# Cross-attention loop with queries turned by VectorE and transfers, projected two steps ahead, and probabilities normalised on ScalarE

## The reference, cut to what matters

```python
x = x + _L0_xattn_ref(_layernorm(x), ctx_2048, mask, ...)   # 16 batches, 128 queries, 128 keys, width 512
x = x + _L0_ffn_ref(_layernorm(x), ...)                     # routed block on 16 rows of each batch
...
q = (hidden_states @ Wq + bq)      # 16 heads of 128
k = (encoder_hidden_states @ Wk + bk); v = ... @ Wv + bv    # 4 heads of 128, each used by 4 query heads
q = _rmsnorm(q, qn_w); k = _rmsnorm(k, kn_w)
scores = einsum('bhsd,bhed->bhse', q, k) / sqrt(128) + attention_mask
out = einsum('bhse,bhed->bhsd', softmax(scores), v)
return out @ Wo
```

## Time and profile before

| | before |
|---|---|
| median of 3 timed runs | 835.98 us (832.25 to 836.52) |
| the profiled execution's own time | 833.15 us |
| its span, first to last instruction | 831.4 us |
| granted TensorE clock, mean | 0.983 of 2.4 GHz |
| busy TensorE, VectorE, ScalarE, GpSimd | 787.2, 566.4, 470.7, 548.3 us |

### The profile page before, as it was taken

The page is one execution under the profiler, slowest core; times in us unless marked ns, Lnnn a source line. Parts: engine busy times, 40 slices in busy tenths (PEclk is TensorE's granted clock), DMA queues, the critical chain, the costliest instruction groups (busy, mean ns, idle before and its releaser), DMA issues. The chain is left out here.

```text
span 831.4 us, 14178 instructions
## 1 busy us (share of the span) xinstructions
PE 787.2 (95%) x3968; PEld 654.6 (79%) x3968; DVE 566.4 (68%) x1049; ACT 470.7 (57%) x1618; POOL 548.3 (66%) x611
## 2 busy tenths in 40 slices
PE   6999996999999999999999999999987799989997
PEld 4888874888888888888888888888865577877886
DVE  4545455687787787787787787778777688754122
ACT  4555455575675675675665665665654256554440
POOL 2333355677777777776776876876867297756980
PEclk9999997999999999999999999999999899999999
DMA  7666663222322332332332332332254655213620
GB/s 231 200 212 205 200 218 97 60 82 68 103 83 68 102 90 64 101 91 67 95 95 63 96 94 63 98 91 63 76 158 155 231 186 182 103 54 125 204 99 25
DMA packets 85001, 97.66 MB, mean 117 GB/s; under 512 B 8112, under 2 KB 48176, under 8 KB 84976
## 3 DMA queue, kind: packets, MB, share of 16 engines
q1 hardware_dynamic: 84400, 95.52, 37.6%
q0 software_dynamic: 576, 1.84, 0.6%
HBM read 63.77 MB, written 17.30 MB: 98 GB/s over the span
## 5 line engine op out<-in xcount | busy, mean ns | idle before, releaser
L900 POOL TENSOR_TENSOR wp_lo<-raw,wp_hi 128x512 fp32r<-128x512 f32 x88 | 113.9, 1336 | 34.8 <-ACT wp_hi L970 34.8
L1080 ACT ACTIVATE p_row<-s_row,neg_max 128x128 f32<-128x128 f32 x256 | 100.0, 395 | 63.8 <-DVE neg_max L1374 63.7
L824 POOL TENSOR_TENSOR p_row<-p_row,p_inv 128x512 f32<-128x512 f32 x64 | 66.8, 1044 | 98.1 <-DVE p_inv L1389 98.1
L1794 PE MATMUL b_y<-wo_hi,oT_hi 128*128 128x512 f32 x256 | 107.5, 420 | 3.4 <-DVE oT_lo L1278 3.4
L1796 PE MATMUL b_y<-wo_hi,oT_lo 128*128 128x512 f32 x256 | 101.8, 398 | 0.0
L1795 PE MATMUL b_y<-wo_lo,oT_hi 128*128 128x512 f32 x256 | 101.8, 398 | 0.0
L1794 PE MATMUL b_q<-wq_hi,xT_hi 128*128 128x512 f32 x248 | 97.8, 394 | 0.0
L1796 PE MATMUL b_q<-wq_hi,xT_lo 128*128 128x512 f32 x248 | 97.4, 393 | 0.0
L1795 PE MATMUL b_q<-wq_lo,xT_hi 128*128 128x512 f32 x248 | 97.3, 392 | 0.0
L970 ACT ACTIVATE oT_hi<-b_o 128x512 fp32r<-128x512 f32 x64 | 38.4, 599 | 102.2 <-PE b_o L1796 100.3
L856 POOL TENSOR_TENSOR pT_lo<-raw,pT_hi 128x512 fp32r<-128x512 f32 x62 | 81.0, 1307 | 0.9 <-ACT pT_hi L970 0.9
(11 more groups left out here) (369 smaller groups left out, 2206.3 us busy)
## 6 DMA issues: line engine op xcount, KB each, us to landing
raw<-raw SPq DMA_DIRECT2D x248, 64.0 KB, 2.1
cx<-in_ctx_dram SPq DMA_DIRECT2D x16, 256.0 KB, 2.7
raw<-in_L_xattn_Wq_dram SPq DMA_DIRECT2D x16, 256.0 KB, 2.7
raw<-in_L_xattn_Wo_dram SPq DMA_DIRECT2D x16, 256.0 KB, 3.2
v_store<-v_out SPq DMA_DIRECT2D x16, 256.0 KB, 3.3
k_store<-k_out SPq DMA_DIRECT2D x16, 256.0 KB, 2.0
xr<-in_x_dram SPq DMA_DIRECT2D x16, 256.0 KB, 3.1
v_raw<-v_store SPq DMA_DIRECT2D x16, 256.0 KB, 3.0
```

What stands on the lines that cost most here:

```text
L824: pool.tensor_tensor(p_row[:], p_row[:], per_head(p_inv, S), ALU.mult).then_inc(p_normed, 1)
L900: last = pool.tensor_tensor(wp_lo[n % NSLOT][:, c, :], raw[RAW_OF[n]][:, c, :], wp_hi[n % NSLOT][:, c, :].bitcast(fp32), ALU.subtract)
L1080: e = act.activation(place, row, ACT.Exp, bias=neg_max[:, h:h + 1], accum_out=p_sum[:, h:h + 1])
L1794: pe.matmul(dst, left[0], right[0], start=start, stop=False)
```

## The change

On TensorE `turn_q` stays for batch 0 only. From quad 4 on, GpSimd's `q_norm` multiplies in place in `q_row`; VectorE's new `q_turn` transposes blocks of 32 x 32 from `q_row` to `q_nrm`; four DMAs of SyncE (`load_q`) put the blocks into one of two places; ScalarE's `loaded_q_high` and GpSimd's new `q_low` split from there. The weight qw moves into the keys' weight. `project_q` works on quad t + 2. The multiplication of the probabilities (`p_norm`) goes from GpSimd (one instruction) to ScalarE (four). x is normalised in place, and `turn_x`, `x_high` and `x_low` move from i = 2 to i = 1. Within a step the order of each queue changes.

```diff
@@ keys are loaded in the layout of the values; SyncE
+                sp.dma_start(k_raw[:], k_store[bass.ds(b * P, P), :].rearrange("(j d) n -> d j n", j=4)
...
+            def load_q(t, par):
+                sp.wait_ge(q_turned, t + 1)
+                for i in range(4):
+                    sp.dma_start(qT_in[par][:, i].rearrange("p h s -> p (h s)"),
+                                 q_tr[32 * i:32 * i + 32].rearrange("d j h s -> d j (h s)")
+                                 ).then_inc(qT_loaded, 16)
...
+                    if (i == NQUAD - 1 or not first) and (i < NQUAD - 1 or not last):
+                        load_q(t + 1, (i + 1) % 2)
                     if not (first and i == 0) and not (last and i == NQUAD - 1):
                         load_p(t - 1, (i - 1) % 2)
@@ GpSimd
+                    pool.tensor_tensor(q_row[:], q_row[:], per_head(q_rs, HD), ALU.mult).then_inc(q_normed, 1)
...
+            def q_low(t, par):
+                pool.wait_ge(qT_hi_done, t + 1)
+                pool.tensor_tensor(by_head(qT_lo), qT_in[par].rearrange("p i h s -> p h i s"),
+                                   by_head(qT_hi).bitcast(fp32), ALU.subtract).then_inc(qT_lo_done, 1)
...
-                    if i == 1 and not last:
+                    if i == 1 and first:
                         x_norm_stat(b + 1)
-                    if i == 2:
+                    if i == 2 and first:
                         v_low(b)
+                    if i < NQUAD - 1 or not last:
+                        q_norm(t + 1)
+                    if i == 1 and not first and not last:
+                        x_norm_stat(b + 1)
                     if i == NQUAD - 1 and not first:
                         out_stat(b - 1)
...
-                    if not (first and i == 0):
+                    if not first:
+                        q_low(t, i % 2)
+                    if i == 2 and not first:
+                        v_low(b)
+                    if last and i == NQUAD - 1:
                         p_norm(t - 1)
                     if not (first and i < 2):
                         p_low(t - 2, i % 2)
-                    if not (first and i < NQUAD - 1) and not (last and i == NQUAD - 1):
-                        q_norm(t + 1)
@@ ScalarE
+            def loaded_q_high(t, par):
+                act.wait_ge(qT_loaded, 64 * (t - NQUAD + 1))
+                wait(act, scored, t)
+                copy(by_head(qT_hi), qT_in[par].rearrange("p i h s -> p h i s")).then_inc(qT_hi_done, 1)
...
+            def p_norm(t):
+                act.wait_ge(p_inverted, t + 1)
+                for h in range(QUAD):
+                    last = act.activation(p_row[:, h, :], p_row[:, h, :], ACT.Copy, scale=p_inv[:, h:h + 1])
+                last.then_inc(p_normed, 1)
...
+                    else:
+                        loaded_q_high(t, i % 2)
...
                         exps(t - 1, last and i == NQUAD - 1)
+                    if i == 2:
+                        v_high(b)
                     if not (first and i < 2):
                         p_high(t - 2, i % 2)
-                    if i == 2 and not last:
+                    if i == 1 and not last:
                         x_high(b + 1)
...
+                    if not (first and i == 0) and not (last and i == NQUAD - 1):
+                        p_norm(t - 1)
+                    if not (first and i < 2) and not (last and i >= 2):
+                        squares(t + 2)
                     if i == NQUAD - 1 and not last:
                         k_high(b + 1)
@@ VectorE
+            def q_turn(t):
+                dve.wait_ge(q_normed, t + 1)
...
+                    dve.wait_ge(qT_loaded, 64 * (t - NQUAD))
+                dve.transpose(q_tr, q_row[:].rearrange("p h (j d) -> p j h d", j=4)).then_inc(q_turned, 1)
...
+                    if (i == NQUAD - 1 or not first) and not (last and i == NQUAD - 1):
+                        q_turn(t + 1)
+                    if not (first and i < 2) and not (last and i >= 2):
+                        q_bias(t + 2, (i + 2) % NQUAD, b_y if first and i == 2 else b_q)
                     if not (first and i == 0):
                         p_invert(t - 1)
...
-                        q_bias(t + 1, (i + 1) % NQUAD)
...
-                        q_low(t)
@@ TensorE
-                        project_q(t + 1, b if i < NQUAD - 1 else b + 1, (i + 1) % NQUAD)
-                    turn_q(t)
+                    if first:
+                        turn_q(t)
...
+                    elif not (last and i >= 2):
+                        project_q(t + 2, b if i < 2 else b + 1, (i + 2) % NQUAD, banks=2 if first else 1)
-                    if i == 2 and not last:
+                    if i == 1 and not last:
                         turn_x(b + 1)
```

More of the change, by code:

```diff
@@ L243, in xattn_then_routed_ffn @@
             tied = sb_in(st, "tied", [P, 1])
+        qT_in = [row.rearrange("p (i h s) -> p i h s", i=4, h=QUAD) for row in (raw[1][:, 3, :], q_in1[:])]
         wo_place.close()
@@ L634, in _ @@
             load_v(0)
-            sp.wait_ge(x_normed, 1)
+            sp.wait_ge(x_turned, 1)
             load_x(1)
@@ L1093, in attend @@
                         o_high(t - 3)
-                    if i == 2:
-                        v_high(b)
-                    if (first and i < NQUAD - 1) or (last and i == NQUAD - 1):
+                    if first:
                         q_high(t)
+                    else:
+                        loaded_q_high(t, i % 2)
                     if first and i < NQUAD - 1:
@@ L1350, in q_bias @@
                 dve.wait_ge(q_projected, t + 1)
-                wait(dve, q_normed, t)
+                if isinstance(t, int) and t <= NQUAD:
+                    wait(dve, q_normed, t)
+                else:
+                    dve.wait_ge(q_turned, t)
                 dve.tensor_tensor(q_row[:].rearrange("p h d -> p (h d)"), bank[:],
@@ L1489, in attend @@
                         norm_out(b - 1)
-                    if first and i == 1:
-                        q_bias(3, 3)
-                    if not (first and i < NQUAD - 1) and not (last and i == NQUAD - 1):
-                        q_bias(t + 1, (i + 1) % NQUAD)
-                    if not (first and i < NQUAD - 1) and not (last and i == NQUAD - 1):
-                        q_low(t)
-                    if i == 2 and not last:
+                    if i == 1 and not first and not last:
                         x_low(b + 1)
-                    if first and i == 1:
-                        dve.wait_ge(w_hi, 2 * NB)
-                        dve.wait_ge(w_lo, 2 * NB)
-                    if not (first and i == 0) and not (last and i == NQUAD - 1):
+                    if not (first and i < 2) and not (last and i == NQUAD - 1):
                         p_turn(t - 1)
@@ L1525, in attend @@
                     s_max(t)
-                    if first and i == 0:
-                        q_bias(2, 2, b_y)
+                    if first and i == 1:
+                        x_low(b + 1)
+                        dve.wait_ge(w_hi, 2 * NB)
+                        dve.wait_ge(w_lo, 2 * NB)
+                        p_turn(t - 1)
+                    if first and i < 2:
+                        q_bias(i + 2, i + 2, (b_y, b_q)[i])
             attend(0, True, False)
@@ L1821, in turn_x @@
                 wait(pe, xT_lo_done, b)
-                turn(b_xT, xn).then_inc(x_turned, 1)
+                turn(b_xT, xr).then_inc(x_turned, 1)
             def kv_project(bank, par, w_hi_, w_lo_, split_at=None):
@@ L1947, in attend @@
                         find_places(0)
[L1948 to L1950 removed]
+                    if first:
+                        turn_q(t)
                     if first and i < 2:
                         project_q(i + 2, 0, i + 2, (b_y, b_q)[i], banks=2)
[L1953 removed]
+                    elif first and i == 2:
+                        project_q(t + 2, b + 1, 0, b_y, banks=2)
+                    elif not (last and i >= 2):
+                        project_q(t + 2, b if i < 2 else b + 1, (i + 2) % NQUAD, banks=2 if first else 1)
+                    if i == 1 and not last:
                         turn_x(b + 1)
```

41 lines of the change are left out of this document (19 added, 22 removed).

## The result

| | before | changed |
|---|---|---|
| median of the timed runs | 836.25 us (4 runs, 832.25 to 837.84) | 907.80 us (4 runs, 906.37 to 910.89) |
| the profiled execution's own time | 833.15 us | 906.69 us |
| its span | 831.4 us | 904.8 us |
| granted TensorE clock, mean | 0.983 | 0.964 |

The changed kernel is slower: ratio 1.0885, 95% interval 1.0845 to 1.0926. The direction was forecast, the size was not: 879 with a range of 850 to 897, and 907.8 lies above it.

What follows compares the result with a forecast made beforehand. TensorE bounds the kernel before, at 31.0 us a batch; after the change a 33.0 us ring of waits does. 833.2 + 28.0 (loop) + 2.0 (batch 15) + 3.6 (batch 0) + 11.9 (clock) = 878.7, forecast 879 us, range 850 to 897.

Steps and rivals of the forecast that it cites:

- TensorE stops being the bound, a ring through all engines takes its place: In the loop, waits across the engines set the batch at 33.0 us, against 29.2 of TensorE's own work.
- `p_norm` 1.18 us: ScalarE's four 128x128 multiplications of the probabilities take 1.18 us, bounds 0.80 and 1.56; they stand in the ring three times.
- The ring of 33.0 us: Closed chain of waits through a batch's four steps, summed to 33.0 us in place of 31.0: 28 us over the loop.
- (a): Ring piece from ScalarE's squares through root, multiplication and row statistic of x, with hand-overs: 4.61 us.
- (b): Ring piece of x_norm (0.69 us), turn_x, add_y and scores to the mask: 5.07 us.
- (d): Ring piece of p_turn, residual and its statistic, three score passes, o_low and norm_out (1.45 us): 6.18 us.
- The clock, 11.9 us: TensorE's idle gaps lower its clock in seven of fourteen loop batches, 1.7 us a fall, about 12 us; ends 0 and 24.
- Batch 0 and the ends: q_norm and v_low delay quad 0's p_low in batch 0, 3.6 us; batch 15 walks the loop's path, about 2 us.
- The prediction's own extreme, 907: p_norm at 1.56 us and one clock fall in each batch: 867 + 16 + 24 = 907 us.
- (1): Rival: the ring holds in the loop but TensorE's clock never falls, 867 us; chance 0.26.
- (2): Rival: TensorE stays the loop's bound and the kernel gets faster, 807 us; chance 0.11.
- (3): Rival: SyncE's queue becomes the bound, load_p waiting behind load_q, 2.50 us a step, about 983 us; chance 0.04.

Runs made afterwards that it cites:

- experiment 1: Changed kernel plus two waits that hold GpSimd's q_low until x_norm (step 1) and until score_wide is written (step 3): 873.08 us, 1.0456 of the kernel before.
- Experiment 2: Changed kernel plus 13 unread matmuls in each loop batch, filling TensorE's gaps to keep its clock up: 906.79 us, 1.0865 of the kernel before.
- experiments 3: Changed kernel with VectorE's reciprocal moved ahead of q_turn and q_bias in each step after batch 0: 882.09 us, 1.0564 of the kernel before.
- experiment 4: Changed kernel with both the two GpSimd waits and VectorE's reciprocal ahead of q_turn and q_bias: 867.35 us, 1.0414 of the kernel before.
- experiment 8: Changed kernel with x_norm and norm_out also writing an unread accumulator, GpSimd not held; output values differ: 880.62 us, 1.0554 of the kernel before.

## Why the prediction was right, and where it failed

- **TensorE stops being the bound, a ring through all engines takes its place** (chance 0.54 and 0.26): right. The waits named as its marks are there: VectorE idles 1.44, 0.87, 1.93 and 1.44 us before the four `p_turn` of a batch, released by ScalarE (the 0.87 is that of step 1, where `x_low` still stands behind the reciprocal and covers a part, which the prediction overlooked), and TensorE's idle notes stand before `turn_x` and `add_y`, 3.8 us a batch (2.52, 1.01 and 0.28), as forecast with 3 to 5; the largest, though, is before the `add_y` of step 0 and not before `turn_x`.
- **`p_norm` 1.18 us**: right. The squares start 1.18 us behind it (446.79 to 447.97). By its rows the prediction had 1.16; the last 0.02 were given no reason and are luck.
- **The ring of 33.0 us**: right as a ring, and 33.27 when nothing collides (experiment 1). (The terms written out in (a) add up to 4.54, not 4.61; the other 0.07 have no row.) The step that failed is the price of two terms in it: in (b) "`x_norm` 0.69 with hand-over (as norm_out's 0.54 us form)", which is 1.55 from its start to that of `turn_x`; and in (d) "`norm_out` 1.45", from its start to `q_turn`, which is 3.08. Both prices were taken from rows in which GpSimd was idle, though the change fills just these idle times of GpSimd. The two terms make 2.5 us a batch, 35 us over the loop.
- **The clock, 11.9 us**: the second step that failed. Falls come in nine of the fourteen batches, where seven were assumed, but at the `add_y` of step 0, which is not in the ring; the prediction had them in (b). Experiment 2 took them away and got nothing back, so the term should have been 0. Its price of a fall in (b), 1.7 us, was about right: 1.5 in experiments 3, 4 and 8, where the falls do stand there. By the advice of the Trainium skill, "TensorE: Matmul & The Clock Gate", Part 1, that was cited there, the term would have been at most 8 us; the changed kernel shows none in the loop.
- **Batch 0 and the ends**: forecast 3.6 for batch 0 and 2.0 for batch 15. Measured 1.5 in batch 0 and 3.9 more in the loop, mostly in its first batch, 0.7 ahead of it, and 1.8 from batch 15 on. Why batch 0 came out cheaper wasn't tried.
- **The sum with the measured sizes**: 833.2 + 65.5 + 3.9 + 1.5 + 0.7 + 1.8 = 906.6, against 906.69 of the profiled execution. This is bookkeeping and proves no cause. It shows that the miss of 29 us hides a larger one: the loop's batches were forecast some 37 us too short, and the clock's 12 us, which never came, hid a part of it.
- **The range**: its upper end, 897, was built from one fall of the clock per batch and a dearer `p_norm`. The unknown that mattered, a pass under other neighbours, had no bound in it. The prediction's own extreme, 907, would have hit the measured time, but by luck: it stands for `p_norm` at 1.56 us and for 24 us of the clock, and neither came.
- **Rivals**: (1), full clock at 33 us and 867, is what experiment 1 brought about (full clock in the loop, 33.27, 873), but the changed kernel itself has both the falls and a longer ring. (2), TensorE stays the bound, did not come. (3), SyncE's queue, was no bound in the changed kernel, but became one as soon as the ring was shorter (experiment 4), through the load of x and not through `load_p`.

## What to carry to other kernels

A duration read from the trace holds only beside the neighbours that it had there: when a change lets GpSimd work where it used to wait, look up which of VectorE's tensor_scalar passes and copies on SBUF stand at that place, and price them once alone and once with the whole of GpSimd's instruction ahead of them. A wait that holds an engine off the critical path can be a gain; here it gained 35 us. And before you charge a fall of TensorE's clock, look up which group is slow and who waits for it: the falls cost nothing in the changed kernel, and 1.5 us each in experiments 3, 4 and 8, where they stood in the ring.

## What was not expected of the hardware

A tensor_scalar pass of 128x512 in float32 takes 0.54 us alone, and 1.50 when GpSimd has started a subtraction on SBUF 0.08 us earlier; the pass with an accumulator takes 0.81 us beside GpSimd and 0.80 alone (experiment 8). A copy of 128x128 goes from 0.23 to 1.25 us in the same way. VectorE's block transposes, 0.70 to 0.71 us, show no such delay in the changed kernel: the one at 472.46 starts 0.05 us behind a pass of GpSimd (472.41) and takes 0.70.
